# Gated cross-attention block with a ternary feed-forward: GpSimd folds two of four softmax key tiles, twelve denominator products per batch instead of sixteen

## The reference, cut to what matters

```python
# x, ctx: (8, 512, 512) float32; 16 heads of 32; hidden width 2048
Q, K, V = heads(linear(layernorm(x), Wq, bq)), heads(linear(ctx, Wk, bk)), heads(linear(ctx, Wv, bv))
qk = einsum('bhqd,bhkd->bhqk', Q, K)
# first pass over the scores: mean, max and variance of softmax(qk / sqrt(32)) per head,
# through a small network -> one temperature t for each batch and head
attn = softmax(qk / (2 * t))                     # second pass
x = x + tanh(g_xattn) * linear(attn @ V, Wo, bo)
x = x + tanh(g_ffn) * ffn(layernorm(x))          # ternary weights, 8-bit activations, gelu
```

## Time and profile before

| | |
|---|---|
| median of three runs | 1318.41 us (1315.38 to 1320.18) |
| profiled execution, its own time | 1316.68 us |
| its span in the trace | 1314.8 us |
| mean granted TensorE clock | 0.969 |
| busy: PE, DVE, ACT, GpSimd | 90%, 82%, 72%, 33% |
| loop, six iterations | some 151 us each |

### The profile page before, as it was taken

The page is one execution under the profiler, slowest core; times in us unless marked ns, Lnnn a source line. Parts: engine busy times, 40 slices in busy tenths (PEclk is TensorE's granted clock), DMA queues, the critical chain, the costliest instruction groups (busy, mean ns, idle before and its releaser), DMA issues.

```text
span 1314.8 us, 23630 instructions
## 1 busy us (share of the span) xinstructions
PE 1182.0 (90%) x6684; PEld 439.9 (33%) x6684; DVE 1075.0 (82%) x1969; ACT 945.6 (72%) x1593; POOL 428.4 (33%) x489
## 2 busy tenths in 40 slices
PE   4866599999999989999999989999999999969988
PEld 2322221444134421444124431344214441224234
DVE  7789689887998879887998879887898879984256
ACT  4688599576985689575985769756895769775833
POOL 3138655321452224530353224511354201220120
PEclk9868789999999999999999999999999999979989
DMA  8822211221112221201212221112112210001000
GB/s 310 227 76 65 57 42 50 49 49 57 32 43 49 58 75 50 49 21 54 57 49 49 55 72 37 32 37 66 65 49 49 49 65 1 1 1 61 5 1 32
DMA packets 36061, 73.81 MB, mean 56 GB/s; under 512 B 8145, under 2 KB 8529, under 8 KB 35409
## 3 DMA queue, kind: packets, MB, share of 16 engines
q1 hardware_dynamic: 35920, 72.13, 19.3%
HBM read 38.39 MB, written 8.39 MB: 36 GB/s over the span
## 4 chain that ended last, share of the span: by engine, by line
PE 58%; DVE 20%; issue 8%; ACT 7%; SPq 2%; DMA 1%; DVEq 1%; POOL 0%; ACTq 0%; POOLq 0%
PE b_ps L1531 10%; PE o_ps L1771 6%; DVE stat L1092 6%; DVE nmax L1082 5%; PE b_ps L1563 5%; PE o_ps L1576 5%; PE z_ps L1587 5%; PE a_ps L1557 5%; PE o_ps L1531 5%; PE z_ps L1531 4%; ACT region L883 3%; PE b_ps L1736 2%; PE z_ps L1771 2%; PE b_ps L1747 2%; ACT etile L851 2%
## 5 line engine op out<-in xcount | busy, mean ns | idle before, releaser
L851 ACT ACTIVATE etile<-a_ps,nmax 128x512 f32<-128x512 f32 x512 | 352.0, 702 | 88.6 <-DVE nmax L1082 88.4
L1082 DVE TENSOR_REDUCE nmax<-a_ps 128x1 f32<-128x512 f32 x512 | 345.3, 679 | 60.5 <-PE a_ps L1557 53.6
L883 ACT ACTIVATE region<-b_ps,inv2t 128x512 f32<-128x512 f32 x512 | 335.0, 704 | 55.0 <-PE b_ps L1563 49.8
L1092 DVE BATCH_NORM_STATS2 stat<-etile 128x6 f32<-128x512 f32 x492 | 335.3, 684 | 14.2 <-ACT etile L851 13.9
L1557 PE MATMUL a_ps<-kst,qst 96*128 96x512 f16 x512 | 197.8, 394 | 31.0 <-ACT etile L851 24.9
L1563 PE MATMUL b_ps<-qst,kst 97*128 97x512 f16 x512 | 193.6, 388 | 13.6 <-DVE region L1322 7.7
L1576 PE MATMUL o_ps<-region,vbuf 128*32 128x512 f32 x1024 | 139.3, 608 | 17.7 <-DVE region L1120 7.1
L1587 PE MATMUL z_ps<-region,ones 128*32 128x512 f32 x1024 | 136.2, 604 | 9.3 <-DVE region L1123 9.3
L749 POOL TENSOR_TENSOR region<-region 128x512 f16<-128x512 f32 x64 | 76.0, 1188 | 195.3 <-ACT region L926 193.9
L1563 PEld LDWEIGHTS b_ps<-qst,kst 97*128 97x128 f16 x512 | 49.5, 97 | 256.8 <-ACT region L883 210.1
L652 POOL TENSOR_TENSOR region<-region 128x512 f32<-128x512 f32 x32 | 40.8, 1276 | 255.0 <-DVE region L1130 255.0
(11 more groups left out here) (332 smaller groups left out, 2002.5 us busy)
## 6 DMA issues: line engine op xcount, KB each, us to landing
kst<-region SPq DMA_DIRECT2D x96, 128.0 KB, 2.3
qst<-region SPq DMA_DIRECT2D x84, 128.0 KB, 2.3
xres<-in_x_dram SPq DMA_DIRECT2D x8, 1024.0 KB, 5.3
out_dram<-xres SPq DMA_DIRECT2D x32, 256.0 KB, 2.0
cin<-in_ctxT_dram SPq DMA_DIRECT2D x30, 256.0 KB, 2.8
cin<-in_x_dram SPq DMA_DIRECT2D x28, 256.0 KB, 2.6
kst<-in_f1T_dram SPq DMA_DIRECT2D x2, 1024.0 KB, 12.0
qst<-in_f2T_dram SPq DMA_DIRECT2D x2, 1024.0 KB, 9.2
```

The source lines that it names most:

```text
L851: nc.scalar.activation(etile[:, k % E_SLOTS, :], a_ps[k % A_BANKS][:, :], ACT.Exp, bias=nmax[:, slot_of(n), t:t + 1], scale=1.0, accum_out ...
L883: nc.scalar.activation(probs[:, (s + 1) % 2, g, :], b_ps[g % 2][:, :], ACT.Exp, scale=inv2t[:, slot:slot + 1]).then_inc(b_exp, 1)
L1082: vec.tensor_reduce(nmax[:, slot_of(k // T), k % T:k % T + 1], a_ps[k % A_BANKS][:, :], AX.X, ALU.max, negate=True).then_inc(a_max, 1)
L1092: vec.bn_stats(stat[:, slot_of(k // T) * T + k % T, :], etile[:, k % E_SLOTS, :]).then_inc(a_stat, covered)
```

## The change

It applies to iterations 1 to 6 (`folded`, equal to `has_p` here); iterations 7 and 8 stay as they were.

- There are four buffers of exponentials, one per key tile: `probs[:, 1]`, `probs[:, 0]`, `region2[:, 0:4]` (otherwise staging for K and a buffer of the feed-forward), and `xres`.
- GpSimd adds the buffer of key tile 1 into that of key tile 0, in place, in one instruction of 128x2048 float32 (`add_sets`). It waits for the exponentials of set 4G+1 and until `values` has read set 4G (`first_read`).
- PE makes three denominator products per group: of the sum (waits `sum_done`), of key tile 2, of key tile 3. They stand in set 4G+3, 4G+4 and 4G+5, behind g = 3. For group 3 the first two stand together in set 15.
- ACT waits in set 4G+4 (G = 0 to 2) until the product of the sum has read the buffer. In set 2 it waits for `tern_pool`, in set 3 for the last store of the batch before.
- DVE's parts 1 and 2 of `normalise` move by one set.
- SP loads `xres` when all sets are used, not when the batch before is stored.
- GpSimd's order is: split_c 0 and 1, add 0, split_c 2 and 3, add 1, split_y 0, normalise_x and split_x of the first pair, add 2, split_y 1, add 3, split_y 2, normalise_x of the second pair.

```diff
+        prob_sets = [probs[:, 1, :, :], probs[:, 0, :, :], region2[:, 0:4, :], xres[:, :, :]]
...
-            def load_res(b):
-                sp_waits.wait_ge(out_done, (b + 1) * 16 * T)
+            def load_res(b, folded):
+                if folded:
+                    sp_waits.wait_ge(set_used, nth(b, SETS, SETS))
+                else:
+                    sp_waits.wait_ge(out_done, (b + 1) * 16 * T)
...
+            def add_sets(b, G):
+
+                first, second = prob_sets[0], prob_sets[1]
+                pool_waits.wait_ge(b_exp, nth(b, H * T, G4 * (T * G + 2)))
+                pool_waits.wait_ge(first_read, nth(b, C, G + 1))
+                pool.tensor_tensor(first, first, second, ALU.add).then_inc(sum_done, 1)
...
-                if has_p and not first:
-                    for c in range(C):
-                        split_c(i + 1, c)
-                if has_b:
+                if has_b and has_p:
+                    split_c(i + 1, 0)
+                    split_c(i + 1, 1)
+                    add_sets(i - 1, 0)
+                    split_c(i + 1, 2)
+                    split_c(i + 1, 3)
+                    add_sets(i - 1, 1)
                     split_y(i - 1, 0)
-                if has_p and not first and not second:
                     normalise_x(i + 1, 0, from_cin)
                     for n in range(2):
                         split_x(i + 1, n, from_cin)
-                if has_b:
+                    add_sets(i - 1, 2)
                     split_y(i - 1, 1)
+                    add_sets(i - 1, 3)
                     split_y(i - 1, 2)
-                if has_p and not first and not second:
                     normalise_x(i + 1, 1, from_cin)
...
-                if g == 0:
+                if g == 0 and not folded:
                     act_waits.wait_ge(set_used, nth(b, SETS, s - 1))
-                nc.scalar.activation(probs[:, (s + 1) % 2, g, :], b_ps[g % 2][:, :], ACT.Exp,
+                elif g == 0 and s >= T and s % T != 1:
+                    act_waits.wait_ge(set_used, nth(b, SETS, s - 2 if s % T == 0 else s - 3))
+                elif g == 0 and s == 2:
+                    act_waits.wait_ge(tern_pool, 2)
+                elif g == 0 and s == 3:
+                    act_waits.wait_ge(out_done, (b + 1) * 16 * T)
+                nc.scalar.activation(prob_sets[s % (T if folded else 2)][:, g, :], b_ps[g % 2][:, :], ACT.Exp,
...
-NORM_AT = ((0, 3), (1, 0), (1, 2))
+NORM_AT, NORM_AT_FOLDED = ((0, 3), (1, 0), (1, 2)), ((0, 3), (2, 0), (2, 2))
...
+            def folded_denominators(b, G, k):
+
+                if k == 1:
+                    if G > 0:
+                        pe_waits.wait_ge(z_out, nth(b, C, G))
+                    pe_waits.wait_ge(sum_done, nth(b, C, G + 1))
+                for g in range(G4):
+                    ins = mat(z_ps[g * DK:(g + 1) * DK, :], ones32[:, 0:DK], prob_sets[0 if k == 1 else k][:, g, :],
+                              start=k == 1, stop=k == T - 1)
+                ins.then_inc(set_used, 2 if k == 1 else 1)
...
-                            if s > 0 and g == 3:
+                            if s > 0 and g == 3 and not has_p:
                                 denominators(i - 1, s - 1)
+                            elif s >= T and g == 3 and s % T < 2:
+                                folded_denominators(i - 1, s // T - 1, 2 + s % T)
+                            elif s % T == T - 1 and g == 3:
+                                folded_denominators(i - 1, s // T, 1)
+                                if s == SETS - 1:
+                                    folded_denominators(i - 1, s // T, 2)
```

More of the change, by code:

```diff
@@ L763, in body @@
                         split_x(i + 1, n, from_cin)
-                if has_b:
+                    add_sets(i - 1, 2)
                     split_y(i - 1, 1)
+                    add_sets(i - 1, 3)
                     split_y(i - 1, 2)
-                if has_p and not first and not second:
                     normalise_x(i + 1, 1, from_cin)
+                elif has_b:
+                    for G in range(C - 1):
+                        split_y(i - 1, G)
+                elif second:
+                    for c in range(C):
+                        split_c(i + 1, c)
                 if first:
@@ L1391, in body @@
                             tile_a(i, set_tiles(i, s)[g])
-                        if has_b and (s % T, g) in NORM_AT and s >= T:
-                            normalise(i - 1, s // T - 1, NORM_AT.index((s % T, g)))
+                        norm_at = NORM_AT_FOLDED if has_p else NORM_AT
+                        if has_b and (s % T, g) in norm_at and s >= T:
+                            normalise(i - 1, s // T - 1, norm_at.index((s % T, g)))
                     if has_p and has_b and s in X_STATS_AT:
@@ L1564, in score_b, with values @@
                     qst[par][0:SHIFT + 1, slot, :], start=True, stop=True).then_inc(b_full, 1)
-            def values(i, has_p, b, par, s):
+            def values(i, has_p, b, par, s, folded):
                 G, k = s // T, s % T
@@ L1576, in values @@
                     ins = mat(o_ps[g * DK:(g + 1) * DK, :], vbuf[par][:, k, n * DK:(n + 1) * DK],
-                              probs[:, (s + 1) % 2, g, :], start=k == 0, stop=k == T - 1)
+                              prob_sets[s % (T if folded else 2)][:, g, :], start=k == 0, stop=k == T - 1)
                 if k == T - 1:
                     ins.then_inc(o_full, 1)
+                elif k == 0 and folded:
+                    ins.then_inc(first_read, 1)
             def denominators(b, s):
@@ L1607, in body @@
                 if has_b:
-                    values(i, has_p, i - 1, 1 - par, SETS - 1)
-                    denominators(i - 1, SETS - 1)
+                    values(i, has_p, i - 1, 1 - par, SETS - 1, has_p)
+                    if has_p:
+                        folded_denominators(i - 1, C - 1, T - 1)
+                    else:
+                        denominators(i - 1, SETS - 1)
                 def tiles_a(point):
```

12 lines of the change are left out of this document (7 added, 5 removed).

## The result

The changed kernel takes **1392.09 us** (median of 4 runs, 1390.92 to 1393.91) against 1318.13 us for the kernel before (4 runs of the same chip): ratio 1.0558, 95% interval 1.0545 to 1.0571. The forecast was 1371, its range 1346 to 1390. The sign and most of the size were right: 53 us were forecast onto 1318, 74 measured. The range was missed by 2 us.

What follows compares the result with a forecast made beforehand. In the sets ACT, PE and DVE were taken as full at once, ACT most. Add 2, add 0 and the clock, 29.7 + 12.2 + 13 = 54.9 us onto 1316.7, gave 1371.6, stated as 1371, range 1346 to 1390.

Steps and rivals of the forecast that it cites:

- Add 2: Addition 2 stands behind the first x pair on GpSimd, so set 12 starts 4.95 us late: 29.7 us in six iterations.
- Add 0: Addition 0 stands behind the splits of context tiles 0 and 1, delaying set 4: 12.2 us in six iterations.
- The clock: PE's waits at set 11 and addition 0 lower its clock: 10 and 3, together 13 us, bounds 0 and 22.
- The price of an addition: One 128x2048 addition on GpSimd: 4.6 us taken, 4.55 by the slope of two rows, 5.10 the upper end.
- What is removed: 24 denominator products, 25.5 us of PE work, don't come off the time; at most ACT's idle 14 us is won.
- The rest, at nothing: Later residual load, K stacking on SP's queue and GpSimd's longer tail cost nothing.
- Adds 1 and 3: Additions 1 and 3 are ready before PE wants them in sets 7 and 15, cover 1.5 us: cost nothing.
- The rival that held it: DVE's reciprocals in sets 6 and 14 are held up by additions 1 and 3: 36 us more, 1407; chance 0.08.
- The third rival: Faster: PE is the true pace-maker, the additions hide and ACT's idle rest is won: 1303 us; chance 0.04.
- Slower: The changed kernel is slower by more than half a per cent; chance 0.94.

Runs made afterwards that it cites:

- guard out: Changed kernel with DVE's floor, reciprocal and comparison of the denominators as one reciprocal instruction: 1371.02 us, ratio 1.0412.
- this part alone: Changed kernel without any addition and with all sixteen groups of denominator products; four buffers, later residual and moved reciprocals stay: 1313.38 us, ratio 0.9961.
- both orders and four pieces: Changed kernel with addition 0 ahead of the splits of c, addition 2 ahead of the x pair, each addition issued as four of 128x512: 1340.20 us.
- addition 2's order alone: Changed kernel with addition 2 and group 1's scaling ahead of the x pair, second x statistics one set later: 1386.38 us, ratio 1.0513.

## Why the prediction was right and where it failed

The way back from the changed kernel goes in three steps, each a measured pair: guard out, 1392.1 to 1371.0; addition 2 ahead of the x pair, to 1329.4; addition 0 ahead of the splits, to 1314.0. The shares hold for this order of the steps: alone, the two orders gave 6 and 13 us.

- **Add 2** (29.7 us, and 10 of the clock): the step is 41.7, the forecast's two terms 39.7. The trace has the parts: set 12 comes 16.07 us after GpSimd's start on the pair, 5.9 later than before, of which 0.9 is the first product at 1.2 GHz. Keeping TensorE busy made it 15.0, the forecast's distance.
- **Add 0** (12.2, and 3 of the clock): the step is 15.3, the trace's own difference 14.7. In the six iterations set 4 comes 9.66 to 9.69 us after the first split where the clock stayed up, 9.8 by the forecast, and 10.74 to 10.77 where it fell.
- **The clock** (13): kept busy before set 11 gave 12.8 by itself, which its scatter doesn't tell from the 10 forecast for it. By its own bounds (-0.6 to +6 for the additions, 0 to 22 for the clock) the sum's range is 1358 to 1387, not 1360 to 1385.
- **The price of an addition** (4.6): 4.52 us, range 4.49 to 4.54. The Trainium skill (GPSIMD Engine Reference, section 3.1) gives 4.497, as near as the 4.55 worked out from the two rows and nearer than the 4.6 taken.
- **What is removed**, at nothing, with 14 us as the most to be won: 4 us with the products left out.
- **The rest, at nothing**: right, and better, as this part alone gains some 5 to 6 us.
- **Adds 1 and 3, at nothing: this is the step that failed.** PE waits for addition 0 in set 3 in all six iterations, 0.65 to 3.2 us (forecast 1 to 4), and sets 7 and 15 don't wait for their sums at all, as forecast. But the step asked only who waits for the addition's result, and costed its presence beside DVE in a rival. The term was 17 to 21 us: that much of the 21 that came back with the guard out is the hold. The kernel with the guard out takes 1371.0, the forecast 1371.6; that they agree to 0.6 us is in part luck, as without the guard up to 3.7 us go that have nothing to do with the hold.

The rival that held it was the right mechanism at the wrong size and chance: 3 us per hold and 36 in all, where the rows show 1.92 and 0.91 us per iteration, 17 in six. It was given 0.08 because of a row: L1127 at 0.18 us beside GpSimd's L673. That row was beside another kind of GpSimd instruction than the additions, and 1.11 us after its start; of a two-input one it says nothing. And two rows above it in the same timeline of the kernel before stands one that spoke for the rival:

```profile
507.46 0.41 DVE L1125 TENSOR_SCALAR zwide<-region 128x16 f32<-128x16 f32 x1
```

The other 26 of that line take 0.17 to 0.18 us, the six beside L673 0.41. They start 0.38 us after L673 (507.08 in iteration 3) and end 0.79 after it.

The rule of the Trainium skill (SBUF - State Buffer, "Who interferes with whom") is borne out where it was set aside: a DVE instruction with two SBUF inputs, or a one-input one that takes both of DVE's port pairs, and a GpSimd instruction that reads SBUF exclude each other for a whole instruction, and one-input instructions outside those modes pass. Here both forms of the floor and the comparison stood until 0.03 to 0.05 us behind the addition's end, and the reciprocal (0.25), the row maximum (from PSUM, 0.69) and the statistics (0.68) beside additions took what they take elsewhere. That the ports are the cause is the page's word; the runs show which forms wait, and that beside an addition the wait ends with the instruction.

The third rival's point ("add 2 must end 8.6 us after GpSimd's start") was never near: it ended 13.4 us after. "Slower" was right with 0.94.

Where the runs differ from the rule: it makes no difference between GpSimd's instructions that read SBUF. Beside the one-input normalisation of 2.08 us (L673, L686 in the changed kernel) what counts is how far it has got. Over all the runs, a floor that starts in its first 0.4 us ends 0.79 us after its start, and one that starts 0.7 to 1.4 us after it takes 0.17 to 0.18. In two single cases a floor that started later was held to its end: 0.50 us in the run with both orders and four pieces (iteration 3), 0.32 in that with addition 2's order alone (iteration 5). The comparison passed it from 0.7 us on. That it has one input isn't the reason, as the CAST above has one too and holds to its end. Why, stays open. A chain that keeps the floor and consists only of instructions that pass wasn't tried either.

## What to carry to other kernels

Work given to an idle engine has two prices: who waits for its result, and who is held while it runs. List the instructions of DVE that fall beside the new GpSimd instruction in time, form by form, and take the proof that they pass only from a row with the same kind on **both** sides, and at the same place within the longer one. Where three waits stand in a row, removing one can bring the next work under another engine's instruction: here a reorder worth 42 us showed 6 until the hold was gone. And before the pricing, take the work out altogether once: 4 us was all that these products were worth.

## What was not expected of the hardware

- A 128x16 instruction of DVE, 0.17 us of work, can stand 4.47 us beside one addition of GpSimd. GpSimd pays nothing that shows: addition 1 takes 4.54 us in the changed kernel, with the floor held beside it, and 4.54 with the guard left out.
- DVE's RECIPROCAL from SBUF to SBUF takes 0.25 us beside an addition and elsewhere, where TENSOR_SCALAR of the same operands is held.
- Four GpSimd additions of 128x512 in a row take 4.92 to 4.97 us and one of 128x2048 takes 4.52. A held DVE instruction gets in between two of them, though no gap shows.
- The length of a wait alone doesn't tell what the clock does. Before set 3, waits of 2.95, 3.14 and 2.24 us (iterations 2, 4, 5) had a granted clock of 0.50 behind them and a product of 1.93 us; one of 3.21 us (iteration 6) left it at 1.00 and the product at 1.06.
